# Three edits in a fused attention, feed-forward and state-space kernel: where score maxima are subtracted, how a 64-row layer is tiled, and at which step a projection stands

## What is computed

```python
# layer 0: a transformer block per image, 1024 positions, 8 heads of 32
x_ln = layer_norm(x_flat, g1, beta1)
q, k, v = split(x_ln @ w_qkv.T)
attn = softmax(q @ k.T * 32 ** -0.5)
y = x_flat + (attn @ v) @ w_proj.T + b_proj
y = y + relu(layer_norm(y, g2, beta2) @ w1.T + b1) @ w2.T + b2   # 64 -> 256 -> 64
# layer 1: two 3x3 convolutions with batch norm, relu and identity
# layer 2: iterative whitening over all images
# layer 3: a selective state space, 128 inner channels, 16 states
xi, z = split(layer_norm(x) @ W_in.T)
xc = silu(causal_conv4(xi))
dt, B, C = split(xc @ W_x.T);  delta = softplus(dt @ W_dt + b_dt)
h[t] = h[t-1] * exp(delta[t] * A) + delta[t] * xc[t] * B[t];  y[t] = sum_n h[t] * C[t]
out = ((y + xc * D) * silu(z)) @ W_out.T + x
```

## Time and profile before

| | us |
|---|---|
| median of 3 runs | 3976.04 |
| lowest and highest | 3971.30 and 3979.86 |
| the profiled execution's own time | 3973.87 |
| its span, first to last instruction | 3972.2 |
| attention, from about 61 to 2122 | 2061 |
| feed-forward and convolutions, from about 2150 to 2498 | 348 |
| state space, loop from about 2707 to 3972 | 1265 |

### The profile page before, as it was taken

How to read it: one execution, slowest core, us unless ns; L and a number is a source line. 1 busy time by engine, 2 the same in 40 slices (tenths; PEclk the granted TensorE clock), 3 DMA queues, 4 the chain that set the end, 5 groups by cost and what they waited for, 6 DMA issues and landing times. The chain is left out here.

```text
span 3972.2 us, 56517 instructions
## 1 busy us (share of the span) xinstructions
PE 3373.5 (85%) x19062; PEld 1207.9 (30%) x19062; DVE 2573.4 (65%) x3346; ACT 2001.1 (50%) x2381; POOL 1924.1 (48%) x620
## 2 busy tenths in 40 slices
PE   6999999999999999999995999657777777777777
PEld 2333333333333333333331333422222222222222
DVE  5677677676676776767750222237777777777777
ACT  3566566565565665656652333234454445444554
POOL 0555566555565655556653000016555655555555
PEclk7899999999999999999997999778888888888888
DMA  2000000000000000000003210134323332333242
GB/s 95 12 14 15 10 17 15 15 15 10 15 17 15 9 15 15 15 15 12 15 9 92 90 63 16 56 103 146 136 96 139 115 130 96 139 115 128 96 143 102
DMA packets 74768, 235.22 MB, mean 59 GB/s; under 512 B 13089, under 2 KB 14181, under 8 KB 74421
## 3 DMA queue, kind: packets, MB, share of 16 engines
q1 hardware_dynamic: 69460, 215.06, 16.0%
q0 software_dynamic: 5056, 16.83, 1.2%
HBM read 192.42 MB, written 39.39 MB: 58 GB/s over the span
## 5 line engine op out<-in xcount | busy, mean ns | idle before, releaser
L526 DVE TENSOR_REDUCE at_pmax<-at_ring 128x1 f32<-128x512 f32 x2048 | 1305.1, 685 | 512.5 <-PE at_ring L334 511.6
L479 ACT ACTIVATE at_probs<-at_sc 128x1024 f32<-128x1024 f32 x1024 | 992.5, 1021 | 660.4 <-PE at_sc L401 660.3
L580 POOL TENSOR_TENSOR at_prob_sums<-at_prob_sums,at_probs 128x2048 f32<-128x2048 f32 x192 | 869.3, 4527 | 109.7 <-ACT at_probs L479 98.7
L398 PE MATMUL at_sc<-at_QT,at_KT 32*128 32x512 f32 x4096 | 847.8, 642 | 21.9 <-issue 21.6
L1634 POOL TENSOR_TENSOR ss_drive<-ss_du,ss_bsb 128x1024 f32<-128x1024 f32 x261 | 610.0, 2350 | 424.9 <-DVE ss_state L1591 417.8
L580 POOL TENSOR_TENSOR at_prob_sums<-at_probs 128x2048 f32<-128x2048 f32 x64 | 291.0, 4547 | 791.2 <-ACT at_probs L479 791.2
L410 PE MATMUL at_O<-at_probs,at_V 128*32 128x512 f32 x4096 | 539.2, 610 | 53.0 <-DVE at_att L549 51.8
L1534 ACT ACTIVATE ss_decay<-ss_delta,ss_a 128x512 f32<-128x512 f32 x520 | 353.2, 687 | 441.8 <-DVE ss_state L1587 304.0
L1423 PE MATMUL ss_Y<-ss_seen,ss_ident 128*128 128x512 f32 x1032 | 540.1, 649 | 0.0
L1599 DVE TENSOR_TENSOR ss_seen<-ss_state,ss_C 128x1024 f32<-128x1024 f32 x259 | 316.3, 1221 | 256.4 <-PE ss_C L1411 249.8
L334 PE MATMUL at_ring<-at_KH,at_QH 32*128 32x512 bf16 x2048 | 447.4, 389 | 5.7 <-DVE at_pmax L526 2.9
(11 more groups left out here) (199 smaller groups left out, 2728.2 us busy)
## 6 DMA issues: line engine op xcount, KB each, us to landing
ss_bsb<-scratch_rows SPq DMA_DIRECT2D x265, 512.0 KB, 6.8
scratch_attn<-at_att SPq DMA_DIRECT2D x64, 256.0 KB, 2.0
fc_att<-scratch_attn SPq DMA_DIRECT2D x32, 512.0 KB, 5.8
ss_xn<-scratch_xm SPq DMA_DIRECT2D x34, 256.0 KB, 5.5
at_xn<-scratch_xn SPq DMA_DIRECT2D x32, 256.0 KB, 3.8
ss_xw<-scratch_xw SPq DMA_DIRECT2D x17, 256.0 KB, 3.7
ln_x<-in_x SPq DMA_DIRECT2D x8, 512.0 KB, 4.4
scratch_xn<-ln_xn POOLq DMA_DIRECT2D x8, 512.0 KB, 3.0
```

What stands on the lines that cost most here:

```text
L398: nc.tensor.matmul(sc[:, h, :], KT[head(h), par, blk(kb)], QT[head(h), par, hs(half)], start=True, stop=False)
L479: nc.scalar.activation(probs[:, kb, two, :].rearrange("p h q -> p (h q)"), sc[:, two, :].rearrange("p h q -> p (h q)"), ACT.Exp, scale=SCA ...
L526: nc.vector.tensor_reduce(pmax[:, quad // 2, h, quad % 2:quad % 2 + 1], ring[:, unit[3], :], AX_X, ALU.max, negate=True).then_inc(max_done, 1)
L580: nc.gpsimd.tensor_tensor(prob_sums[:, half, :, :], before, probs[:, k, :, :], ALU.add).then_inc(pool_sums, 1)
```

## The change

In `scores` the two one-row products of heads 0 and 1 are moved ahead of the scores of heads 2 and 3, with their signal. `hidden` takes only the 64 rows that hold an image's weights, one image in rows 0 to 63 into `fc_B` and one in rows 64 to 127 into `fc_A`, and goes by halves of the hidden channels; the second half waits for both relus of the first, and ScalarE's relus are renamed to fit. `AT_X` becomes 6 (`AT_CONV` is used nowhere).

```diff
@@ scores
-                for h in range(GH):
-                    row = slice(h * DH, h * DH + 1)
-                    m = nc.tensor.matmul(sc[:, h, :], ones_bf[row, :], nrow[row, half, :], start=False, stop=True)
                     if h % 2:
+                        for of in (h - 1, h):
+                            row = slice(of * DH, of * DH + 1)
+                            m = nc.tensor.matmul(sc[:, of, :], ones_bf[row, :], nrow[row, half, :], start=False, stop=True)
                         m.then_inc(sc_ready, 1)
@@ hidden
-                for t in range(2 * M):
-                    dst = (B, A)[t % 2]
-                    if t > 1:
-
-                        pe.wait_ge(relu_done, (2 * i + u) * 2 * M + t - 1)
+                for m in range(M):
+                    if m:
+                        pe.wait_ge(relu_done, (2 * i + u) * 2 * M + 2 * m)
                     for h in range(2):
-                        m = nc.tensor.matmul(dst[u][:, hs(h)], w1[:, t // M, (t % M) * P:(t % M + 1) * P], yn[:, u, hs(h)],
-                                             start=True, stop=True)
-                    m.then_inc(ff1_done, 1)
+                        for b, dst in enumerate((B, A)):
+                            k = nc.tensor.matmul(dst[u][:, hs(h)], w1[rows(b), b, m * P:(m + 1) * P], yn[rows(b), u, hs(h)],
+                                                 start=True, stop=True)
+                            if h:
+                                k.then_inc(ff1_done, 1)
@@ deviations_and_hidden
-                    nc.scalar.activation(hid[:, u, t // M, t % M, :], (B, A)[t % 2][u][:], ACT.Relu,
-                                         bias=b1c[:, t % M:t % M + 1]).then_inc(relu_done, 1)
+                    nc.scalar.activation(hid[:, u, t % 2, t // 2, :], (B, A)[t % 2][u][:], ACT.Relu,
+                                         bias=b1c[:, t // 2:t // 2 + 1]).then_inc(relu_done, 1)
@@ state_space_phase
-        AT_X, AT_CONV, AT_Z, AT_BC, AT_REST, AT_MID, AT_DT, AT_LOW, AT_DELTA = 3, 4, 8, 9, 10, 11, 12, 12, 13
+        AT_X, AT_CONV, AT_Z, AT_BC, AT_REST, AT_MID, AT_DT, AT_LOW, AT_DELTA = 6, 6, 8, 9, 10, 11, 12, 12, 13
```

## The result

| | before | after |
|---|---|---|
| median, us | 3974.7 (4 runs) | 3761.8 (4 runs, 3755.7 to 3765.3) |
| ratio, 95% interval | | 0.9462 (0.9444 to 0.9479) |
| profiled execution, span | 3972.2 | 3754.0 |
| first to last exponential of attention | 2009.9 | 1952.1 |
| feed-forward, first to last product | 345.0 | 347.6 |

The change takes 213 us, where 176 were forecast. Of the difference of the two profiled spans, 218 us, the state space has 159 and attention 58; the feed-forward stage is 2.5 longer, and 4 lie between the stages.

A forecast was written before the change was run, and what follows sets the result against it. Bounds by stage: attention's loop of ScalarE exponentials and TensorE scores, TensorE in feed-forward, VectorE in the state space. Gains 128 + 48 + 0 = 176 from 3973.9 gave 3798, forecast as 3799; range 3755 to 3840 (0.61), wider 3735 to 3880.

The forecast's parts named there:

- State space, 128 forecast: Projection moved three steps back: 8.0 us gained per image over 16 images, 128 us; ends 78 and 186.
- the 7 us wait: State space: TensorE's 7.06 us wait for the next image's `ss_xn`, claimed to go to nothing with the projection in step 6.
- the new hole: State space, step 7: VectorE waits for the spread delayed by the moved projection; 2.7 us an image.
- the case at 2.4 GHz: State space: with the projection at full clock, VectorE's hole at step 7 is almost nothing, 0.1 to 0.3 us.
- The gain of 0.4 at step 8: State space: step 8 follows busy passes, so some of its 2.0 us hole goes, 0.4 us an image.
- Attention, 48 forecast: Row products moved ahead: 1.55 us gained a period over 31 to 32 periods, 48 us; ends 0 and 109.
- The loop of two steps: Attention, ordinary steps: scores, values and exponentials take 5.68 us for two steps, 2.84 a step against 3.18.
- Feed-forward, 0 forecast: Hidden layer 6.1 us against 7.07, set against a possible slow clock behind a new idle stretch; ends +7.6 and -20, taken as 0.
- In order: Rival, attention: scores of heads 2 and 3 wait behind row products, about 160 us lost, 4006 us; chance 0.04.
- VectorE takes the gain: Rival, attention: clumped maxima make VectorE last everywhere, so attention gains nothing, 3846 us; chance 0.13.
- Slow clock everywhere: Rival: projection at 1.2 GHz in all images (78), feed-forward -20, attention 48, giving 3868 us; chance 0.15.
- Everything overlaps: Rival: projection at full clock (165 to 186), attention 95, feed-forward 7, about 3695 to 3710 us; chance 0.07.

## Why the prediction was right, point by point

The time, 3761.8, lies in the range of 3735 to 3880 and in the forecast's own range of 3755 to 3840, 37 us below the forecast of 3799.

**State space, 128 forecast, 159 measured (166 alone, in time).** The mechanism held: the 7 us wait went, VectorE's wait for the spread fell further than named (80 us, not 120), the units of steps 8 to 12 lost nothing. The count was one too high: in 15 images VectorE has the hole of 10.3 us, not in all 16. In image 0 TensorE did not wait, the projection took 3.60 us and the hole was 0.19. So 8.0 an image should have been 120 us, and 159 were measured. The term that was mis-sized is the new hole, 2.7 us an image. It came from one choice, the slow clock in two thirds of the images at step 6, read off step 8. The clock there was full in all 16 images and the hole 0.0; the case at 2.4 GHz in the same paragraph said 0.1 to 0.3. The reasoning took light steps with idle stretches of 1.47 as the cause of step 8's slow clock. In the kernel after three such steps ahead of the projection, TensorE busy 6.76 of 11 us, have

```profile
2925.00:2936.00 11.00, 6.76 (x19) 2.40 (x18) 10.53 (x10) 4.15 (x6) 6.27 (x3) 1.00 1.02 329
```

a granted clock of 1.00, and the kernel with step 7 has all its projections at 3.6 us behind four. What made step 8 slow is open. One difference before was the hole, 7 us of waiting in 15 images, which this edit removes. But of these 15 only ten had the slow step 8, and in the kernel with the projection in step 5 three images had it with a wait of 1.03 us or none. The forecast carried the clock of one place over to another without a row for that. The gain of 0.4 at step 8 was too small as well (its holes, up to 2.0 in 11 images, went altogether: 25 us with those of the step behind), and part of it came back at step 13, where a slow stretch now lies in every image:

```profile
2889.70:2900.00 10.30, 10.27 (x14) 3.76 (x15) 6.90 (x6) 8.04 (x10) 5.73 (x3) 0.50 0.96 366
```
```profile
2899.12 1.22 DVE L1600 TENSOR_TENSOR ss_seen<-ss_state,ss_C 128x1024 f32<-128x1024 f32 x1 [3.12 <-PE ss_C L1412]
```

The holes of step 13 add up to 35 us instead of 26. By VectorE's line the account closes: -155 at the old hole, -25 behind step 8, +9 at step 13, +1 at step 2, +10 for the decay: -160. ScalarE's `take_x` was costed at nothing, and the waits for the decay don't speak against that. They stand at step 10, 1.0 an image, in all 16 images now. Before, they stood in images 0, 1, 9, 10, 11 and 13, which are image 0 and the five without a hole behind step 8, and the kernel with step 5 has them in exactly the 13 images without that hole. So they take back part of the gain at step 8.

**Attention, 48 forecast, 58 measured (59 alone).** The loop of two steps was forecast at 5.68 and is 5.66. The ordinary period was to lose 1.55 us and lost 1.55 (61.45 to 59.90), with the pairs 2.50 and 3.16 apart where 2.5 and 3.2 were named. 31 of them are 48 us. The other 8 to 10 us are in the periods around a turn of the outer loop (twelve that lose 1.9 on average), in the first two (2.3 and 3.7) and in the last but one (2.4). At such a turn TensorE stands still for some 3.5 us, and in five of six turns the slow stretch behind got shorter, 6.8 instead of 10.2 us. First row before, second after:

```profile
984.70:994.90 10.20, 9.17 (x37) 3.36 (x41) 3.63 (x6) 3.13 (x4) 0.00 (x0) 0.51 0.01 2
```
```profile
961.30:968.10 6.80, 6.80 (x26) 2.25 (x26) 3.83 (x6) 3.13 (x4) 0.00 (x0) 0.51 0.00 0
```

I had not looked at these. ScalarE's wait for the scores fell by 103 us, not by 50: 41 of them came back as longer waits of its copies for the ring (13.7 for the sums, 20.6 for the values of step 6, 6.5 for K), and the net 62 is about the stage's 58. What I had named was the net gain, put down to one line. That 48 came so near is in part luck: by the profiles of the kernels with this attention the gain is anything from 49 to 59.

**Feed-forward, 0 forecast, 0 measured (3.5 us slower alone, interval -2 to +10).** Here the steps held one by one: the half of 1.8 us, the second half 4.2 us behind the first (2191.33 to 2195.52), an idle stretch of 2.1 (2.20), and a clock of 0.50 for 3.4 us behind it. Without the slow stretch an interval is 1.0 us shorter than before, as costed (0.95), with it 0.7 longer (0.95 - 1.7).

**The rivals.** "In order" did not happen: the row products of heads 0 and 1 hold nothing up (997.89 to 998.85 above). The Trainium skill, TensorE: Matmul & The Clock Gate, Part 2, holds that matmuls stay in program order; here the trace does not agree for the starts, since four of the eight passes from 997.89 on stand behind the row products of 998.85 in the program. With maxima in their place the scores do come late, and that kernel's attention is 203 us longer than before, where the rival had 160; but the cause is another, VectorE's bank. "VectorE takes the gain" did not happen in the plain steps: VectorE's reductions still wait 454.8 us for TensorE (508.7 before), and these steps have the length that was worked out without it. Whether the longer steps 4, 6, 9 and 12 are its doing is not shown.

```profile
DVE at_pmax L526 <- PE at_ring L334: 454.8, 420, 5.7
```

"Slow clock everywhere" came true in the feed-forward stage alone. "Everything overlaps" (3695 to 3710) came nearest for the state space (159 against 165 to 186, of which the lower end is 155 over 15 images) and was wrong for the other two.

## What to carry to other kernels

When you take a clock from a row to price a moved step, it is the clock of that place in that kernel: ask what else the change alters ahead of it, and look for a row of the moved work itself. The kernel before had one, the projection of image 0 that waited for nothing and took 3.60 us. An idle stretch of 2 us inside a busy TensorE stage cost its length and the slow clock behind it here (2.1 + 1.7 us), and filling it with other products got both back. Before a product with a wait is moved ahead of others, work out when that wait is met in its new place: the row products, with no wait or a met one, were passed by the scores behind them, and the maxima, whose bank VectorE frees only 1.1 us after the first scores, held them. When an interval fits the end of one operation to 0.01 us, look at a step where another engine is late before calling it the cause.

## What the runs showed of the hardware that I had not expected

- One-row products and scores of other rows pass each other, and a met wait on them changes nothing (0.22 us between the pairs of heads with and without it). A wait that is not met holds the scores behind it, on other rows too: in the three kernels with the maxima in this place they start 1.25 us behind the first pair in plain steps and 1.84 where VectorE is later, each time 0.13 us after its signal.
- Three steps in a row with TensorE busy 6.76 of 11.0 us had a granted clock of 1.00, and the projection behind three or four such steps took 3.6 us in all 16 images, in the kernels with step 6 and step 7 alike. Yet step 8 was at 0.50 in ten of 15 images of the kernel before, and behind two such steps in three images of the kernel with step 5. The cause is open. A single stretch of 2.20 us in a stage otherwise without a gap was followed by 0.50 for 3.4 us in five of eight places, and in none once it was filled.
- A stage that an edit doesn't touch can move by 5 to 10 us: the state space in the kernel with attention's edit alone by 9.5, and attention by 6 and 8 in the two kernels that filled the hidden layer or moved the output projection.
